# An eight-layer hybrid kernel: how one stage ends and the next begins (semaphore clears, reload of x, LayerNorm statistics)

## The chip, the cores and the metric

The kernel runs on one core of one Trainium2 chip. The metric is the device time of one execution in microseconds (us), as a median over several runs; lower is better. Five engines work side by side and meet by semaphores: PE (TensorE, the matrix unit), DVE (VectorE), ACT (ScalarE), POOL (GpSimd) and SP (SyncE, which here only issues DMAs).

## The reference

One chain of eight layers on x, 8 batches of 1024 rows with 256 elements each, all float32. Every layer adds its result to x and starts from a LayerNorm of x:

```python
x = x + _L0_attn_a_ref(_layernorm(x), ...)   # local attention
x = x + _L0_ffn_ref(_layernorm(x), ...)      # top-128 rows for each of 8 experts, two GEMMs, scatter-add
x = x + _L0_attn_b_ref(_layernorm(x), ...)   # spectral attention (DFT over 64 rows, attention, convolution)
x = x + _L0_ffn_ref(_layernorm(x), ...)      # the same experts again
x = x + _L1_attn_a_ref(_layernorm(x), ...)   # second-order linear attention
x = x + _L1_ffn_ref(_layernorm(x), ...)      # tanh(h @ W @ A1 @ A2 + bias)
x = x + _L1_attn_b_ref(_layernorm(x), ...)   # window attention
x = x + _L1_ffn_ref(_layernorm(x), ...)
```

`_layernorm` subtracts the mean of a row and divides by `sqrt(var + 1e-5)`. In the expert layer a router scores every row for 8 experts, each expert takes its best 128 rows of a batch, and `out` is added back to these rows (`.at[...].add(out)`).

## The kernel before, in words

**Stages.** The layers run one after the other, each as one stage, the two expert layers as two: `la` (local attention), `m2r` and `m2e` (router and experts), `sp` (spectral attention), `m4r` and `m4e`, `so` (second-order attention), `t6` (tanh), `wa` (window attention), `t8` (tanh, writes the output). Each is one `nc.Block()`, in which every engine has a program of its own and which ends in a barrier of all five engines. No engine enters the next stage before the last one is done.

**x and its statistics.** x stays in SBUF as `R.X`, 64 tiles (NT) of 128 rows, 8 tiles (TB) to a batch. LayerNorm is made in three steps. While a stage adds its result, DVE takes `bn_stats` of each finished tile into `R.raw` (6 numbers per row). At the start of the next stage `layernorm_scales` (L73 to L88) works on all 64 tiles at once: seven small DVE instructions, a square root on ACT (L93, behind an ACT_TABLE_LOAD), then the reciprocal and `R.shift` on DVE. Then `scaled` is counted up, and ACT or POOL normalise tile by tile.

**Experts.** The scatter-add works on a copy of x in DRAM, `sum_dram`. So `la` and `sp` store x there batch by batch (SP, counted in `x_out`), and at the end of their program SP waits until all eight stores have landed (L2424 closes the block in `la`; L909 is the store in `sp`). `m2e` runs 32 steps of pairs of batches (PAIRS = 32, 4 pairs for each of 8 experts; pair s % 4 holds batches 2s and 2s+1) in a skewed pipeline: in each step DVE first adds the second bias to item t-5 (`add_b2`, L750), weighs the same item (`weigh`, L758), and takes statistics of item t-8 (`stats`, L767). POOL scatters an item (L624) as soon as it is weighed. SP reloads `R.X` batch by batch (L593) once a batch has been scattered by all 8 experts. `stats` does something only for items 28 to 31, so all 64 `bn_stats` stand behind the last `weigh`. At the end POOL waits for all scatters.

**Semaphores.** Semaphores are scarce, so a stage hands its own back. `Stage.__exit__` (L118 to L122) does it with a second block, with its own barrier, in which POOL clears every semaphore of the stage one by one, and the other engines wait: 28 after `m2r`, 21 after `m2e` and 7 more in yet another block, 73 after `sp`, 36 after `m4r`, 21 and 7 after `m4e`, 45 after `so`, 29 after `wa`. `la`, `t6` and `t8` keep theirs and have no such block.

**What follows.** `sp` opens with twelve copies of weights, then a loop over b = -1 to 7: in step b the scores of batch b+1 are masked and reduced by DVE (L1360, L1364), exponentiated by ACT (L1184), and x of batch b+2 is normalised by ACT (L1153). `so` loops over 258 steps t; in each, DVE masks the scores (`mask_AB`, L1887) and, one item behind, `mask_P` (L1895), on which PE waits at L1677; POOL normalises two tiles ahead (L1931).

## Time and profile before

| what | us |
|---|---|
| median of 3 runs | 3836.1 (3835.32 to 3837.97) |
| the profiled execution, its own time | 3835.71 |
| its span, first to last instruction | 3833.9 |
| PE busy | 3505.2 (91%) |
| DVE busy | 2365.9 (62%) |
| ACT busy | 2113.1 (55%) |
| POOL busy | 1465.5 (38%) |
| mean granted TensorE clock | 0.962 of full speed |

The time of an execution is its span and 1.8 us around it. "Idle before, releaser" in a row is the time that the engine stood idle ahead of that instruction and what it waited for; "PEq L118" is the barrier of a clearing block (PE's queue was the last event seen), "PEq L176" and "PEq L2424" that of a block without one.

### The profile page before, as it was taken

What the parts mean: (1) busy time and instruction counts of PE and PEld (TensorE: products, weight loads), DVE (VectorE), ACT (ScalarE), POOL (GpSimd) and SP (SyncE); (2) the same over time, 40 slices, a digit from 0 to 9 for tenths busy, and PEclk for the clock granted to TensorE, in tenths of its full rate; (3) what the DMA queues carried; (4) which work ended last, traced back from release to release, by engine and by line L of the source; (5) the groups of instructions that cost most, each with busy time, mean ns of one, the idle gap of its engine ahead of it and who ended that gap; (6) DMA issues with size and microseconds to landing.
All of it is one profiled execution on the core that took longest, in us unless ns stands there. A gap on an engine that the chain in (4) does not pass through costs nothing. (4 is left out here: it accounts for less than half of the span.)

```text
span 3833.9 us, 115714 instructions
## 1 busy us (share of the span) xinstructions
PE 3505.2 (91%) x44514; PEld 3084.7 (80%) x44514; DVE 2365.9 (62%) x6483; ACT 2113.1 (55%) x6525; POOL 1465.5 (38%) x2245
## 2 busy tenths in 40 slices
PE   8948999699838999699999999999988999999998
PEld 7838999577728999699899999999976777777777
DVE  6774555588764554544444444444446888888894
ACT  3345555355445555244444444444444888888895
POOL 3444665201024665244444444444444222222215
PEclk9969999799969999899999999999999999999999
DMA  3133443411143443300000000000000000000002
GB/s 121 45 134 97 92 92 75 125 46 51 51 167 98 94 94 71 99 3 3 3 3 3 3 3 3 3 3 3 3 6 16 2 2 2 2 2 2 2 2 93
DMA packets 137901, 164.62 MB, mean 43 GB/s; under 512 B 11392, under 2 KB 127264, under 8 KB 137376
## 3 DMA queue, kind: packets, MB, share of 16 engines
q1 hardware_dynamic: 112800, 123.81, 10.0%
q0 software_dynamic: 24576, 33.57, 5.3%
q8 instruction: 359, 5.88, 0.6%
q14 instruction: 166, 1.36, 0.1%
HBM read 97.18 MB, written 60.16 MB: 41 GB/s over the span
## 5 line engine op out<-in xcount | busy, mean ns | idle before, releaser
L2249 ACT ACTIVATE wa_S<-wa_S,wa_top 128x256 f32<-128x256 f32 x1024 | 511.6, 506 | 138.9 <-DVE wa_top L2313 138.0
L1887 DVE TENSOR_TENSOR so_raw<-so_rows,so_masks 128x1024 f32<-128x1024 f32 x256 | 313.5, 1225 | 228.3 <-PE so_rows L1589 220.7
L2313 DVE CUSTOM_DVE_ANT_0 wa_S<-wa_bank,wa_band 128x256 f32<-128x256 f32 x1024 | 366.9, 420 | 8.4 <-issue 8.2
L1951 POOL TENSOR_TENSOR so_more<-so_compact,so_head 128x384 f32<-128x384 f32 x224 | 185.2, 827 | 337.2 <-PE so_bankC L1671 307.0
L2172 PE MATMUL wa_bank<-ident,wa_S 128*128 128x128 f32 x2048 | 273.9, 275 | 22.2 <-ACT wa_probT L2256 22.2
L2172 PEld LDWEIGHTS wa_bank<-ident,wa_S 128*128 128x128 f32 x2048 | 230.3, 141 | 67.1 <-ACT wa_S L2249 31.2
L1876 DVE SCALAR_TENSOR_TENSOR so_compact<-so_compact,so_bankX 128x96 f32<-128x96 f32 x192 | 48.8, 254 | 363.2 <-PE so_bankX L1707 363.2
L1805 ACT COPY so_O<-so_bankC 128x128 f32<-128x128 f32 x256 | 68.2, 266 | 307.6 <-PE so_bankC L1671 307.5
L1956 POOL TENSOR_TENSOR so_OT<-so_O,so_OT 128x128 fp32r<-128x128 f32 x256 | 117.1, 457 | 307.9 <-ACT so_OT L1811 307.9
L703 ACT ACTIVATE m4e_hT<-m_bank,m4e_bias 128x256 fp32r<-128x256 f32 x256 | 126.3, 493 | 152.2 <-PE m_bank L655 145.0
L703 ACT ACTIVATE m2e_hT<-m_bank,m2e_bias 128x256 fp32r<-128x256 f32 x256 | 126.4, 494 | 149.3 <-PE m_bank L655 142.8
L1618 PE MATMUL so_bankJ<-so_xnT,so_w 128*128 128x256 f32 x1500 | 206.6, 287 | 1.5 <-DVE so_xnT L1868 1.5
L2249 ACT ACTIVATION_READ_ACCUMULATOR wa_S<-wa_S,wa_top 128x1 f32 x1024 | 199.3, 195 | 0.0
L2321 DVE COPY wa_probT<-wa_bank 128x512 f32<-128x512 f32 x256 | 167.1, 687 | 47.8 <-PE wa_bank L2172 46.5
L655 PE MATMUL m_bank<-m4e_exT,m_w_parts 128*128 128x256 f32 x1536 | 190.5, 283 | 1.1 <-issue 1.1
L2082 POOL COPY wa_share_all<-wa_share 128x256 f32<-128x256 f32 x64 | 25.4, 396 | 434.6 <-DVE wa_share L2328 434.6
L655 PE MATMUL m_bank<-m2e_exT,m_w_parts 128*128 128x256 f32 x1536 | 189.9, 283 | 0.4 <-ACT m2e_h L703 0.4
L669 PE MATMUL m_bank<-m_w_parts,m4e_hT 128*128 128x256 f32 x1536 | 189.5, 282 | 0.6 <-DVE m4e_pre L750 0.6
L669 PE MATMUL m_bank<-m_w_parts,m2e_hT 128*128 128x256 f32 x1536 | 189.5, 282 | 0.6 <-DVE m2e_pre L750 0.6
L669 PEld LDWEIGHTS m_bank<-m_w_parts,m2e_hT 128*128 128x128 f32 x1536 | 186.3, 188 | 0.8 <-issue 0.8
L669 PEld LDWEIGHTS m_bank<-m_w_parts,m4e_hT 128*128 128x128 f32 x1536 | 186.3, 188 | 0.8 <-issue 0.8
L655 PEld LDWEIGHTS m_bank<-m4e_exT,m_w_parts 128*128 128x128 f32 x1536 | 184.7, 190 | 1.3 <-issue 1.3
(450 smaller groups left out, 10201.4 us busy)
## 6 DMA issues: line engine op xcount, KB each, us to landing
m_w_raw<-in_L_ffn_W_dram SPq DMA_DIRECT2D x64, 512.0 KB
sum_dram<-X SPq DMA_DIRECT2D x16, 1024.0 KB, 5.0
X<-sum_dram SPq DMA_DIRECT2D x16, 1024.0 KB, 6.5
X<-in_L_attn_a_x_dram SPq DMA_DIRECT2D x8, 1024.0 KB, 11.8
xn_dram<-m2r_xn SPq DMA_DIRECT2D x16, 512.0 KB, 3.7
sp_gx<-gate_dram SPq DMA_DIRECT2D x64, 128.0 KB, 2.9
xn_dram<-m4r_xn SPq DMA_DIRECT2D x16, 512.0 KB, 3.8
out_dram<-X SPq DMA_DIRECT2D x8, 1024.0 KB, 4.4
```

What stands on the lines that cost most here:

```text
L655: last = nc.tensor.matmul(bank[:, 0:2 * P], w_parts[:, par, a, c, f * P:(f + 1) * P], exT[:, s % 2, b, c], start=(n == 0), stop=(n == len( ...
L669: last = nc.tensor.matmul(by[u][:, 0:HID], hT[:, s % 2, a, f, u * P:(u + 1) * P], w_parts[:, par, b, 2 + f // QF, f % QF * HID:(f % QF + 1 ...
L703: last = nc.scalar.activation(to, bh[f % 4][:, 0:2 * P], ACT.Gelu_apprx_tanh, bias=bias[:, par, f:f + 1])
L1618: last = nc.tensor.matmul(bank[:, 2 * k * P:2 * (k + 1) * P], w[:, a, n, c, cols], xnT[:, b, c], start=(m == 0), stop=(m == 2 * len(PARTS) ...
L1805: nc.scalar.copy(O[:, t % UT], bC[:, P:2 * P]).then_inc(s_["O_copied"], 1)
L1887: nc.vector.tensor_tensor(AB[:, t % 2].rearrange("p h m t -> p h (m t)"), rows4[:, :, 0:2 * P], masks[:].rearrange("p m t -> p (m t)")[:, ...
L1951: nc.gpsimd.tensor_tensor(state[:, t % UT], compact[:, t % UT, :, None, :].broadcast_to([P, 3, HG, DK]), head[:, None, :, None].broadcast_ ...
L1956: nc.gpsimd.tensor_tensor(OT[:, 1, t % (2 * UT)], O[:, t % UT], OT[:, 0, t % (2 * UT)].bitcast(F32), ALU.subtract).then_inc(s_["O_ready"], 1)
L2172: last = nc.tensor.transpose(bT[q % 2][:, (2 * h + k) * P:(2 * h + k + 1) * P], S[:, n % 2, 2 * q + h, k * P:(k + 1) * P], R.ident[:])
L2249: nc.scalar.activation(S[:, n % 2, z], S[:, n % 2, z], ACT.Exp, bias=top[:, n % 2, z:z + 1], scale=-1.0, accum_out=sums[:, i % 2, SET * c ...
L2313: nc.vector.tensor_tensor_reduce(out=S[:, n % 2, z], in0=bS[g][:, eo * SPAN:(eo + 1) * SPAN], in1=band[:], scale=-(D ** -0.5), scalar=3e38 ...
L2321: nc.vector.tensor_copy(probT[:, n % 2, 2 * q:2 * q + 2].rearrange("p h k t -> p (h k t)"), bT[q % 2][:]).then_inc(s_["T_dve"], 1)
```

## The change

**Clears move.** `Stage.__exit__` makes no block any more. It puts the stage's semaphores on a list, and an engine of the next stage clears them in its own program by `Stage.clear_finished`: POOL in `m2r` (38, those of `la`, now a Stage too), DVE at the start of `m2e` and `m4e` (28, 36), POOL in `sp` before it zeroes `XK` (20), POOL in `m4r` (72), POOL in `so` (20; behind its waits for `loaded` and `scaled`, ahead of its first tile), POOL in `t6` (45), `wa` (12) and `t8` (29).

**The stores of x are awaited late.** `x_out` is no longer a stage's own, SP does not wait for it, and POOL waits for it at the start of `m2e` and `m4e`.

**The experts' end.** SP reloads only batches 0 to 5 in the experts' stage; 6 and 7 stand at the end of the next stage's list of loads. POOL no longer waits for all scatters. `stats` has delay 7 and acts for items 28 and 29 only, so the experts' stage takes statistics of batches 0 to 3. The rows of indices and `y`, from which the last scatters read, are no longer a stage's own.

**Late statistics.** LayerNorm is done in halves. The start of `sp` and `so` works on tiles 0 to 31 (`FIRST`). For tiles 32 to 63 (`REST`): in `sp`, DVE does 32 `bn_stats` and the seven small instructions in one piece ahead of its loop (b = -1), ACT the square root at b = 0, DVE reciprocal, shift and `R.diff` at b = 1, and ACT waits for it at b = 2. In `so`, DVE does one `bn_stats` in each of steps 16 to 47, between `mask_AB` and `mask_P`, the seven at t = 48 and the last ones at t = 50, ACT the square root at t = 49, and POOL waits for it before tile 32.

```diff
+def fetch_result(sp, R, b, before):
+    sp.wait_ge(R.scattered[b], (before + 1) * 16 * 8)
+    sp.dma_start(R.X[:, b * TB:(b + 1) * TB, :],
+                 R.sum_dram[b * SEQ:(b + 1) * SEQ, :].rearrange("(j p) d -> p j d", p=P)).then_inc(R.row_back[b], 16)
...
+    @staticmethod
+    def clear_finished(eng):
+        for sems, sem_ctx in Stage.finished:
+            for s in sems:
+                eng.sem_clear(s)
+            Stage.cleared.append(sem_ctx)
+        Stage.finished.clear()
+
     def __exit__(self, *error):
-        if not error[0] and self.sems:
-            with self.nc.Block() as block:
-                @block.gpsimd
-                def _(pool):
-                    for s in self.sems:
-                        pool.sem_clear(s)
+        for sem_ctx in Stage.cleared:
+            sem_ctx.close()
+        Stage.cleared.clear()
+        Stage.finished.append((self.sems, self.sem_ctx))
         return self.ctx.__exit__(*error)
...
-                    for b in range(BATCH):
-                        sp.wait_ge(scattered[b], 16 * E + scattered_before)
-                        sp.dma_start(R.X[:, b * TB:(b + 1) * TB, :],
-                                     summed[b * SEQ:(b + 1) * SEQ, :].rearrange("(j p) d -> p j d", p=P)).then_inc(row_back[b], 16)
+                    for b in range(BATCH - 2):
+                        fetch_result(sp, R, b, before)
...
+                    pool.wait_ge(R.x_out, 16 * BATCH * (before + 1))
                     skewed(pool, PAIRS, [(0, fetch), (3, scatter)], unroll=U)
-                    for b in range(BATCH):
-                        pool.wait_ge(scattered[b], 16 * E + scattered_before)
...
-                        if isinstance(t, int) and t >= PAIRS - PE_:
+                        if isinstance(t, int) and PAIRS - PE_ <= t < PAIRS - 2:
...
-                    skewed(dve, PAIRS, [(3, split_xT), (4, split_h), (5, add_b2), (5, weigh), (0, split_w), (8, stats)], unroll=U)
+                    Stage.clear_finished(dve)
+                    skewed(dve, PAIRS, [(3, split_xT), (4, split_h), (5, add_b2), (5, weigh), (0, split_w), (7, stats)], unroll=U)
...
+                for b in range(BATCH // 2, BATCH):
+                    dve.wait_ge(R.row_back[b], 16)
+                    for j in range(TB):
+                        ins = nc.vector.bn_stats(R.raw[:, b * TB + j, :], R.X[:, b * TB + j, :])
+                c.then(ins)
+                variances(nc, c, R, var_ready, REST)
                 for b in range(-1, BATCH):
                     u = STEPS * b
                     attend, read = b + 1 < BATCH, b + 2 < BATCH
+                    if b == 1:
+                        dve.wait_ge(std_ready, 2)
+                        scales(nc, c, R, REST)
...
+                    if STATS_AT <= t < STATS_AT + NT // 2:
+                        late = t - STATS_AT + NT // 2
+                        dve.wait_ge(R.row_back[late // TB], 32)
+                        ins = nc.vector.bn_stats(R.raw[:, late, :], R.X[:, late, :])
...
                 pool.wait_ge(s_["loaded"], 5 * 16)
                 pool.wait_ge(s_["scaled"], 1)
+                Stage.clear_finished(pool)
```

In the lists that follow, each row is an instruction (or a run of equal ones) in the order of one engine's program. A semaphore in brackets has the name of the first stage that used the same hardware semaphore, so it may read like that of another stage.

DVE at the end of `m2e`, first before, then with the change:

```order
L750 TENSOR_TENSOR m2e_pre<-m_bank,m_b 128x256 [waits m2e_y_ready,m2e_down_done]
L750 TENSOR_TENSOR m2e_pre<-m_bank,m_b 128x256 [waits m2e_y_ready]
L758 TENSOR_SCALAR m2e_y<-m2e_pre,m_gate 128x256 [waits scattered2,m2e_pre_ready]
L758 TENSOR_SCALAR m2e_y<-m2e_pre,m_gate 128x256 [waits scattered3,m2e_pre_ready]
L767 BN_STATS raw<-X 128x6 [waits m2e_row_back0]
L767 BN_STATS raw<-X 128x6 x7
L767 BN_STATS raw<-X 128x6 [waits m2e_row_back1]
```

```order
L759 TENSOR_SCALAR y<-m2e_pre,m_gate 128x256 [waits scattered1,m2e_pre_ready]
L768 BN_STATS raw<-X 128x6 [waits row_back0]
L768 BN_STATS raw<-X 128x6 x7
L768 BN_STATS raw<-X 128x6 [waits row_back1]
...
L751 TENSOR_TENSOR m2e_pre<-m_bank,m_b 128x256 [waits m2e_y_ready,m2e_down_done]
...
L759 TENSOR_SCALAR y<-m2e_pre,m_gate 128x256 [waits scattered3,m2e_pre_ready]
L768 BN_STATS raw<-X 128x6 [waits row_back2]
...
L768 BN_STATS raw<-X 128x6 [waits row_back3]
...
L587 UNCONDITIONAL_BRANCH
L1331 UNCONDITIONAL_BRANCH [waits barrier_Pool_Activation_PE_DVE_SP_release]
L76 TENSOR_TENSOR mean<-raw 128x32
```

Sixteen statistics now stand ahead of the last `add_b2`, sixteen behind it, and then DVE is in `sp`.

POOL from the end of `m4e` to its first tile of `so`, before and with the change. The second list's `m2_q_loaded2,m2_b2_ready` are `loaded` and `scaled` of `so`:

```order
L624 DMA sum_dram<-m4e_y,m4e_rows 8192x256 x2
...
L122 ISA x21
L118 UNCONDITIONAL_BRANCH
L119 UNCONDITIONAL_BRANCH [waits barrier_Pool_Activation_PE_DVE_SP_gather]
L122 ISA x7
L118 UNCONDITIONAL_BRANCH
L1923 UNCONDITIONAL_BRANCH [waits barrier_Pool_Activation_PE_DVE_SP_gather]
L1931 TENSOR_SCALAR so_xn<-X,rstd,shift 128x256 [waits sp_g_stored,sp_q_done]
```

```order
L626 DMA sum_dram<-y,rows 8192x256 x2
L587 UNCONDITIONAL_BRANCH
L1960 UNCONDITIONAL_BRANCH [waits barrier_Pool_Activation_PE_DVE_SP_gather]
L137 ISA [waits m2_q_loaded2,m2_b2_ready]
L137 ISA x19
L1971 TENSOR_SCALAR so_xn<-X,rstd,shift 128x256 x2
```

The 28 clears between barriers are gone; 20 stand between the wait for `loaded` and the first tile.

ACT in `sp`, from the end of step b = -1 to the exponential of step b = 0, with the change:

```order
L1213 ACTIVATE sp_gel<-sp_acc 128x8x28 [waits la_pT_ready]
L103 ACT_TABLE_LOAD
L103 ACTIVATE var<-var 128x32 [waits sp_var_ready]
L1157 ACTIVATE sp_xn<-X,shift,rstd 128x256 [waits sp_f_done] x8
L1188 ACT_TABLE_LOAD
L1188 ACTIVATE sp_late<-sp_late 128x1024 [waits sp_shifted]
```

The two rows at L103 are new; the rest stood there before (as L1209, L1153 and L1184).

## Rows read from the trace of the kernel before

**Rows 1.** Timeline, DVE: a block that ends in its barrier alone (t6 to wa).
```profile
2922.55 0.27 DVE L77 TENSOR_TENSOR mean<-raw 128x64 f32<-128x64 f32 x1 [0.30 <-PEq L176]
```
**Rows 2.** Timeline, end of m2e, start of sp; then PE at the start of so.
```profile
686.14 0.76 DVE L750 TENSOR_TENSOR m2e_pre<-m_bank,m_b 128x256 f32<-128x256 f32 x2 [5.32 <-PE m_bank L669]
687.34 21.00 DVE L767 BATCH_NORM_STATS2 raw<-X 128x6 f32<-128x256 f32 x64
710.93 0.27 DVE L77 TENSOR_TENSOR mean<-raw 128x64 f32<-128x64 f32 x1 [2.60 <-PEq L118]
...
1572.60 8.75 PE L1712 MATMUL so_bankC<-ident 128*128 128x128 f32 x60 [24.83 <-PEq L118]
```
**Rows 3.** Timeline, first instructions of m2e, m4e, t6 and t8 behind clears.
```profile
291.21 0.21 DVE L726 TENSOR_SCALAR m2e_bias<-m_b 128x8 f32<-128x8 f32 x1 [2.36 <-PEq L118]
...
1149.54 0.21 DVE L726 TENSOR_SCALAR m4e_bias<-m_b 128x8 f32<-128x8 f32 x1 [3.16 <-PEq L118]
...
2846.80 0.27 DVE L77 TENSOR_TENSOR mean<-raw 128x64 f32<-128x64 f32 x1 [3.75 <-PEq L118]
...
3753.42 0.27 DVE L77 TENSOR_TENSOR mean<-raw 128x64 f32<-128x64 f32 x1 [2.71 <-PEq L118]
```
**Rows 4.** Timeline, start of m2r, behind la's last store of x.
```profile
235.90 0.17 DVE L484 MEMSET m2r_ones<- 128x128 f32 x1 [3.38 <-PEq L2424]
...
238.99 0.29 PEld L373 LDWEIGHTS m_bank<-ident,m2r_wg_rows 8*128 8x128 f32 x2 [9.46 <-DMA m2r_rowbase<-in_row_base_dram]
```
**Rows 5.** Timeline, end of sp and start of m4r.
```profile
1083.76 0.38 SPq L909 DMA_DIRECT2D sum_dram<-X  x1
...
1086.09 0.18 ACT L1238 COPY L<-sp_bank 128x32 f32<-128x32 f32 x1 [0.42 <-PE sp_bank L1082]
...
1093.58 1.28 ACT L93 ACT_TABLE_LOAD   x1 [7.31 <-PEq L118]
```
**Rows 6.** Timeline, what stands idle where clears go: DVE in m2e, POOL before m4e.
```profile
301.74 0.69 DVE L732 CAST m2e_exT<-m_bank 128x512 fp32r<-128x512 f32 x1 [10.33 <-PE m_bank L640]
...
1149.53 0.20 POOL L606 TENSOR_TENSOR m4e_rows<-m_index,m_zero 128x2 uint32<-128x2 uint32 x1 [7.86 <-POOLq L118]
```
**Rows 7.** Reload of x in m2e: two issues in the timeline, and landing times.
```profile
685.11 2.22 SPq L593 DMA_DIRECT2D X<-sum_dram  x2
...
DMA to landing us min/median/max: 5.6/7.0/7.9
```
**Rows 8.** Timeline, sp: the first ACT instruction and step b = -1.
```profile
715.80 0.20 ACT L1242 ACTIVATE sp_alpha<-sp_alpha 128x1 f32<-128x1 f32 x1 [0.85 <-DMA sp_alpha<-_L_attn_b_alpha_raw_dram]
...
744.33 0.69 DVE L1360 SCALAR_TENSOR_TENSOR sp_late<-sp_bank,sp_mask 128x512 f32<-128x512 f32 x1 [9.90 <-PE sp_bank L988]
...
747.21 1.23 DVE L1364 TENSOR_TENSOR sp_late<-sp_late,sp_tops 128x1024 f32<-128x1024 f32 x1
...
750.75 1.04 ACT L1184 ACTIVATE sp_late<-sp_late 128x1024 f32<-128x1024 f32 x1
```
**Rows 9.** Timeline, sp, step b = 0: PE behind the normalise, and a table load.
```profile
770.90 2.14 PE L927 MATMUL sp_bank<-sp_dft,sp_xn 128*128 128x128 f32 x16 [1.36 <-ACT sp_xn L1153]
...
774.19 1.28 ACT L1184 ACT_TABLE_LOAD   x1
```
**Rows 10.** Timeline, so: POOL's first tile, then one step of the loop.
```profile
1582.15 1.09 POOL L1931 TENSOR_SCALAR so_xn<-X,rstd,shift 128x256 f32<-128x256 f32 x2 [29.23 <-DMA so_head<-in_head_dram]
...
1659.72 0.68 DVE L1895 TENSOR_TENSOR so_raw<-so_rows,so_masks 128x512 f32<-128x512 f32 x1
...
1661.30 0.43 PE L1677 MATMUL so_bankU<-so_raw,so_KW 128*32 128x128 f32 x8
```
**Rows 11.** Windows: us, then busy of PE, PEld, DVE, ACT, POOL; PEclk, DMA share, GB/s.
```profile
717.00:723.00 6.00, 5.87 (x27) 5.90 (x28) 1.76 (x3) 3.53 (x7) 1.59 (x3) 0.50 1.08 367
...
1613.00:1670.00 57.00, 57.00 (x1092) 52.73 (x1085) 27.20 (x42) 26.05 (x91) 28.55 (x45) 1.00 0.01 3
```
**Rows 12.** The page's row of the granted TensorE clock, in 40 slices.
```profile
PEclk9969999799969999899999999999999999999999
```

More of the change, by code:

```diff
@@ new lines, in scales, with layernorm_scales, std_of_var @@
+def scales(nc, c, R, tiles=slice(0, NT)):
+    c.then(nc.vector.reciprocal(R.rstd[:, tiles], R.var[:, tiles]))
+    c.then(nc.vector.tensor_tensor(R.shift[:, tiles], R.mean[:, tiles], R.rstd[:, tiles], ALU.mult))
+def layernorm_scales(nc, dve, R, step, var_ready, std_ready, tiles=slice(0, NT)):
+    c = Chain(dve, step)
+    variances(nc, c, R, var_ready, tiles)
+    dve.wait_ge(std_ready, 1)
+    scales(nc, c, R, tiles)
+    return c
+def std_of_var(nc, act, R, var_ready, std_ready, tiles=slice(0, NT), count=1):
+    act.wait_ge(var_ready, count)
+    nc.scalar.activation(R.var[:, tiles], R.var[:, tiles], ACT.Sqrt).then_inc(std_ready, 1)
@@ L570, in top_k_experts @@
             bias_ready = ex.sem("bias_ready")
-            row_back = [ex.sem(f"row_back{b}") for b in range(BATCH)]
             bx, bh, by = ban[0], ban[1:5], ban[6:8]
@@ L891, in _ @@
                 sp.dma_start(wg_rows[:], A["L0_ffn_Wg"]).then_inc(wg_loaded, 16)
+                for b in range(BATCH - 2, BATCH):
+                    fetch_result(sp, R, b, 0)
                 for b in range(BATCH + 1):
@@ L1522, in second_order_attention @@
         s_ = {n: sem(n) for n in names}
+        FIRST, REST = slice(0, NT // 2), slice(NT // 2, NT)
+        STATS_AT = 4 * UT
         def tile(t):
@@ L1564, in _ @@
                     sp.dma_start(to, C[name]).then_inc(s_["loaded"], 16)
+                for b in range(BATCH - 2, BATCH):
+                    fetch_result(sp, R, b, 1)
             @block.tensor
@@ L2736, in hybrid_kernel @@
 def hybrid_kernel(nc, A, C, out):
+    Stage.finished.clear()
+    Stage.cleared.clear()
     with ExitStack() as ctx:
@@ L2745, in hybrid_kernel @@
         R.fetched = [sem(f"fetched{n}") for n in range(4)]
+        R.row_back = [sem(f"row_back{b}") for b in range(BATCH)]
+        R.x_out = sem("x_out")
+        R.rows, R.y = sb("rows", [P, BATCH, 2], U32), sb("y", [P, 2, 2, HID])
         R.scattered = [sem(f"scattered{b}") for b in range(BATCH)]
```

111 lines of the change are left out of this document (56 added, 55 removed).

## The prediction, made before the change was run

> **What bounds the kernel now.** I read the windows first. In the loop of `so`, PE is busy for 57.00 of 57.00 us while DVE works for 27.20 and the DMA engines for 1% [rows 11]; over the whole span PE is at 91% (the table of times). Inside the stages PE is the bound and nothing in the change makes its work shorter. So I went to the places where PE stands still, and read the timeline around each change of stage: the reader is to look at the time in brackets, idle time ahead of the first instruction. At the start of `so` PE had been idle for 24.83 us, and its releaser is a barrier [rows 2]. These seams are what the change can win.
>
> **The price of a bare barrier and of a clear.** t6 to wa has no clearing block, and DVE starts 0.30 us after its last instruction [rows 1]. Where 28, 36 and 45 semaphores are cleared in between, the idle time is 2.36, 3.16 and 3.75 us [rows 3]. With two barriers (0.6) taken off that is 1.76/28 = 0.063, 2.56/36 = 0.071 and 3.15/45 = 0.070 us for a clear; I take 0.067.
>
> **Savings at the plain seams.** Each falls to a bare 0.30: m2r to m2e 2.36 - 0.30 = 2.1; m4r to m4e 3.16 - 0.30 = 2.9; so to t6 3.75 - 0.30 = 3.45; wa to t8 2.71 - 0.30 = 2.4 [rows 3]. Together 10.85.
>
> **la to m2r.** DVE idles 3.38 us behind its last instruction, since SP holds the barrier until the last store of x has landed [rows 4]. Without that wait 3.38 - 0.30 = 3.1. But PE in `m2r` first waits for a load, `m2r_rowbase` [rows 4], and the loads are now issued while 1 MB is still being stored. I take 2.7 (1.8 to 3.1).
>
> **sp to m4r.** The last store is issued at 1083.76, the last work on ACT ends at 1086.27, and ACT goes on at 1093.58, after 7.31 us: the landing of the store, then 73 clears at 0.067 = 4.9 [rows 5]. All goes but 0.3: 7.0.
>
> **End of the experts, twice.** DVE ends its statistics at 687.34 + 21.00 = 708.34 and begins `sp` at 710.93 [rows 2]; one of them costs 21.00/64 = 0.328. Sixteen now stand ahead of the last `add_b2`, where DVE was idle for 5.32 us: 16 x 0.328 = 5.25, hidden. Their reloads are long there, since item 29 was scattered 11 us earlier. Sixteen follow the last `weigh`: 687.34 + 5.25 = 692.6. POOL issues its last scatter until 691.3 and no longer waits. So `sp` begins at 692.6 + 0.3 = 692.9 instead of 710.93, and nearly the same rows stand at the end of m4e: about 17.9 each, 35.8 for both.
>
> Sum of savings: 10.85 + 2.7 + 7.0 + 35.8 = 56.35 us.
>
> **Where clears are put.** In `m2e` and `m4e` DVE does 28 and 36 at the start (1.9 and 2.4 us), ahead of an idle time of 10.33 us [rows 6]. In `m2r` 38 on POOL take 2.5 us while the scales are being made, some 3.2 us. In `m4r` 72 take 4.8, about 1.4 later than `scaled`, but POOL had been idle for 7.86 us at that stage's end [rows 6] and only writes `xn`: 0 (up to 1.4 if the last store of `xn` then lands after DVE's index work). In `sp`, `t6`, `wa` and `t8` POOL has nothing due in that time. In `so` there is no cover: the 20 clears stand between `loaded` and POOL's first tile, which now starts the moment that `so_head` has landed [rows 10], with PE waiting on it: 20 x 0.067 = 1.3.
>
> **Costs at the start of sp.** SP queues its loads while the reload of batches 4 and 5 (issued at 685.11 and after, 7 us to landing [rows 7]), the scatters of 6 and 7, and then their reload are under way. ACT's first instruction waits on a load [rows 8]. I add 0.5 (0 to 2). In step b = -1, DVE must put 32 x 0.328 = 10.5 and seven small instructions (at some 0.23 each, less than the 0.27 of [rows 2], 1.6) into the 9.90 us in which it waits for the first scores [rows 8]: 2.2 too long. But DVE's last step there ends at 748.44 and ACT, which takes it, is busy until 750.75 [rows 8], so 2.3 of delay fit: 0.2 (0 to 2.3). In step b = 0 ACT gets the square root and a table load (1.28 as in [rows 9], and 0.26) ahead of its normalise, on which PE already waits for 1.36 [rows 9]: 1.55. DVE's three instructions at b = 1: 0.5 (0 to 1). Sum 2.75.
>
> The row of the table load shows 1.28 us at 774.19, and the exponential that needs it starts at 775.49, right behind it [rows 9]. The Trainium skill, "ScalarE: Activation LUTs", section "What ACT_TABLE_LOAD costs", gives about 1283 ns and a drain of about 1380 ns, 2.66 us for a switch. By that page the sum would be 1.4 us higher, and the time 3786; the trace shows no drain behind this one.
>
> **Costs in so.** Its loads meet the same reloads: 1.0 (0 to 2). The clears: 1.3. The late statistics: one `bn_stats` before `mask_P` in 32 of 258 steps. `mask_P` (L1895) ends at 1660.40 and PE takes it at 1661.30, with no idle time of its own [rows 10], so 0.9 us of slack stand against 0.33. The bound from above is that PE was ready for it: 32 x 0.33 and the 2.7 of the small instructions = 13. The chain of seven at t = 48 and three at t = 50, 1.6 and 1.1 us at once, is over the slack: 0.5. Sum 2.8.
>
> **Net.** 56.35 - 2.75 - 2.8 = 50.8. The profiled execution took 3835.7, so 3784.9; the median lies 0.4 above it: **3785 us**.
>
> **Rivals.**
> (A) As above, 3785, its own range 3783 to 3792. For it: every saving is read from a barrier's own idle time, and PE is the engine that waits there.
> (B) All costs hidden: the loads land in time and the slack in `sp` and `so` holds. Only the 20 clears and the table load remain, 2.9 us: 3836.1 - 56.35 + 2.9 = 3782.7, and with 3.1 for la, 3782. With nothing exposed at all it is 3779.8.
> (C) The change doesn't do what it says: a block still ends only when the DMAs that its engines issued are done. Then la loses its 2.7, sp to m4r the landing (2.0), and each end of the experts runs on to the landing of the last scatters, some 2.5 later: about 10 us, 3795. Against it: the instruction lists show nothing but the barrier there. For it: no row of before shows a barrier with a DMA under way, since t6 has none [rows 1].
> (D) The late statistics are not hidden but only moved. In `sp` the reload of batch 7 comes late and the whole block of 12 us lies on the path; in `so` the 32 cost their 13. That is 24 us: 3809. Against it: the slack in [rows 8] and [rows 10], and DVE at 27.20 of 57 [rows 11].
> (E) Slower than before: PE's clock. At the start of `so` PE does a burst of 60 transposes of the identity, 8.75 us at 1572.60 [rows 2], and then idles until POOL's first tile at 1582.15 [rows 10], 2 us. The clears and the crowded loads lengthen this to some 4.3 us. PE is busy without a pause in the loop behind it [rows 11], so if the granted clock fell from 2.4 to the 1.2 GHz level there and stayed, each us of PE's work would take two: the gain is gone once that lasts for over 51 us of its work, and 80 us would give 3785 + 80 = 3865. Against it: at the start of `sp`, after a pause far longer, the clock stood at 0.50 for 6 us (717 to 723) and the loop of `so` ran at 1.00 [rows 11]; in the page's row no slice of 96 us lies below 0.6 and each one that does lie at 0.6 is followed by 0.9 [rows 12].
>
> The same with rows alone: if the pause of 4.3 us does lower the clock and it comes back as in `sp`, 6 us at 0.50 cost 3 us, and the time is 3788, inside A. The Trainium skill, "TensorE: Matmul & The Clock Gate", section "HAM oscillation — how this bites in real kernels", speaks against this part of the change: a wait for a DMA between two bursts lets the array fall back to half its clock, and the next burst starts cold. The short pause of before did not do that lastingly, for the loop runs at 1.00 [rows 11]; no run here shows the longer one.
>
> **Chances.** A 0.73, B 0.10, C 0.07, D 0.06, E 0.04. The likeliest is A, 3785. The range takes in the bounds: all costs at their lower end give 3779.8; the small ones at their upper end (2 + 2.3 + 1.55 + 1 in `sp`, 2 + 1.3 + 1 in `so`, 1.4 in `m4r`, 0.9 for la) are 13.5 in place of 5.6 and give 3793, and C gives 3795. With a us or two for the price of a clear: 3778 to 3797. A measurement of this kernel can tell about 0.2% (8 us) from no change. Faster by more than that: A, B, C and nearly all of D (at 3809 it is still 27 us faster), 0.94. Within: 0.03, the clock low for some 50 us, or D with losses of its kind in other stages. Slower: 0.03, the rest of E.
>
> **What the profile after would show.** Right: DVE's idle time before its first LayerNorm instruction (the L77 of before) near 0.3 at every change of stage; 16 `bn_stats` in the gap before the last `add_b2`; `sp` beginning some 7 us after that `add_b2`, not 25; PE still at 57 of 57 in the loop of `so`. C is seen in a barrier wait of 2 us and more where x was stored. D is seen in DVE waiting for `row_back` in `sp`, and in PE waiting for `so_raw` at L1677 in steps 16 to 47. E is seen in a granted clock near 0.5 behind the burst and into the loop. The forecast falls with whichever of them is the larger: 24.83 us of PE's idle time before `so` that shrink by less than 17, or a loss of over 8 us inside `sp` or `so`.

## The result, and the profile after

The changed kernel takes 3797.5 us (median of 4 runs, 3795.73 to 3799.22) beside 3836.6 us (4 runs, 3835.32 to 3837.97): a ratio of 0.990, 95% interval 0.9888 to 0.9913. It is 39.1 us faster. The prediction said 3785, and its range, 3778 to 3797, ended half a microsecond below the measured time. The direction was right, the size was 12 us too large.

The profiled execution has a span of 3793.8 us, 40.1 below the 3833.9 of before. The start of each stage is the first LayerNorm instruction on DVE (for `m2r` and `m4r` the memset ahead of it, for `m2e` and `m4e` POOL's first instruction). From start to start, in us, with the change that the prediction's terms add up to:

| stage | before | changed | measured | forecast |
|---|---|---|---|---|
| up to m2r (la) | 235.9 | 233.1 | -2.8 | -2.7 |
| m2r | 55.3 | 53.3 | -2.0 | -2.1 |
| m2e | 419.7 | 407.0 | -12.8 | -17.9 |
| sp | 382.8 | 377.5 | -5.3 | -4.3 |
| m4r | 55.9 | 54.4 | -1.4 | -2.9 |
| m4e | 423.1 | 411.3 | -11.8 | -17.9 |
| so | 1274.2 | 1275.2 | +1.0 | -0.7 |
| t6 | 75.8 | 74.0 | -1.7 | 0 |
| wa | 830.9 | 827.3 | -3.6 | -2.4 |
| t8 | 80.5 | 80.7 | +0.2 | 0 |
| sum | | | -40.1 | -50.8 |

So the gap is at the two ends of the experts' stages (11.2 of it), in `m4r` (1.5) and in `so` (1.7); elsewhere 3.7 came on top.

The seams that carry nothing but a barrier now do what was forecast. Timeline of the changed kernel, first instructions of `m2r`, `m4r`, `t6` and `t8` (start, us, instruction, idle time before it and what ended it; they answer to [rows 3 to 5]):

```profile
233.14 0.17 DVE L488 MEMSET m2r_ones<- 128x128 f32 x1 [0.36 <-PEq L2464]
...
1070.76 1.28 ACT L103 ACT_TABLE_LOAD   x1 [0.27 <-PEq L883]
...
2811.77 0.28 DVE L76 TENSOR_TENSOR mean<-raw 128x64 f32<-128x64 f32 x1 [0.32 <-PEq L1578]
...
3713.11 0.28 DVE L76 TENSOR_TENSOR mean<-raw 128x64 f32<-128x64 f32 x1 [0.30 <-PEq L2077]
```

The 3.38, 7.31, 3.75 and 2.71 us of before are 0.36, 0.27, 0.32 and 0.30.

The end of `m2e` does not. Timeline of the changed kernel, DVE, then SP, then POOL, answering to [rows 2]:

```profile
676.32 5.32 DVE L768 BATCH_NORM_STATS2 raw<-X 128x6 f32<-128x256 f32 x16
681.66 0.76 DVE L751 TENSOR_TENSOR m2e_pre<-m_bank,m_b 128x256 f32<-128x256 f32 x2
...
682.86 5.32 DVE L768 BATCH_NORM_STATS2 raw<-X 128x6 f32<-128x256 f32 x16
693.41 0.22 DVE L76 TENSOR_TENSOR mean<-raw 128x32 f32<-128x32 f32 x1 [5.24 <-PEq L587]
...
680.62 2.28 SPq L109 DMA_DIRECT2D X<-sum_dram  x2
...
685.24 1.55 POOL L626 DMA_INDIRECT sum_dram<-y,rows  x1 [0.30 <-issue]
693.38 0.15 POOL L1479 MEMSET sp_wgT<- 128x64 f32 x1 [6.60 <-POOLq L587]
```

The sixteen statistics fit into the gap ahead of the last `add_b2`, as forecast, and DVE is done at 688.18. Then everybody waits: SP has issued its last reload at 682.9, POOL its last scatter at 686.79, and the barrier opens at 693.4. DVE idles for 5.24 us where 0.3 was forecast, and the end of `m4e` shows 5.38. In windows of 1 us the traffic stops before the barrier opens (us, then busy time of PE, PEld, DVE, ACT, POOL, granted clock, DMA share, GB/s):

```profile
689.00:690.00 1.00, 0.00 (x0) 0.00 (x0) 0.00 (x0) 0.00 (x0) 0.00 (x0) 0.50 1.19 250
690.00:691.00 1.00, 0.00 (x0) 0.00 (x0) 0.00 (x0) 0.00 (x0) 0.00 (x0) 0.50 0.74 131
691.00:692.00 1.00, 0.00 (x0) 0.00 (x0) 0.00 (x0) 0.00 (x0) 0.00 (x0) 0.50 0.08 12
692.00:693.00 1.00, 0.00 (x0) 0.00 (x0) 0.00 (x0) 0.00 (x0) 0.00 (x0) 0.50 0.00 0
```

The trace also names who is late. At a block's end it has an instruction named `DRAIN` for an engine, and the barrier opens when the last of these has ended. Neither a timeline nor the lists of instructions above show it, but the view of one line does (L587 here is the barrier of the experts' block; the numbers are the duration in ns, three times the same, then the start in us). The changed kernel:

```profile
L587 SPq DRAIN  x1: 123/123/123, 683.0 to 683.0; - x1
L587 POOLq DRAIN  x1: 10145/10145/10145, 683.0 to 683.0; - x1
L587 DVEq DRAIN  x1: 3922/3922/3922, 684.3 to 684.3; - x1
```

SP's takes 0.12 us, although two of its reloads have not landed. DVE's ends at 688.2, with its statistics. POOL's ends at 693.1, 6.3 us after its last instruction, and the barrier opens behind it. At the end of `m4e` it ends 6.5 us after.

At the start of `so`, PE after its burst, and POOL ahead of it (answering to [rows 2, 10]):

```profile
1536.56 8.56 PE L1735 MATMUL so_bankC<-ident 128*128 128x128 f32 x60 [11.94 <-PEq L587]
...
1548.54 1.10 POOL L1971 TENSOR_SCALAR so_xn<-X,rstd,shift 128x256 f32<-128x256 f32 x2 [18.76 <-issue]
...
1549.79 0.71 PE L1634 MATMUL so_bankJ<-ident,so_xn 128*128 128x128 f32 x4 [4.67 <-POOL so_xn L1971]
...
1552.02 2.93 PE L1641 MATMUL so_bankJ<-so_xnT,so_w 128*128 128x256 f32 x12 [1.53 <-DVE so_xnT L1893]
```

POOL's first tile comes 11.98 us after the stage's start instead of 9.55, PE's pause is 4.67 us instead of 2.04, and the twelve matmuls at 1552.02 take 2.93 us.

### The profile page after: what moved, and what is told of

Its sections match the earlier page's. It is cut to its first block and busy times, and to the rows that moved or that the text cites. A ratio compares the mean times of both kernels' runs of the same rounds, so it can differ in the third digit from the quotient of the medians.

```text
span 3793.8 us, 115662 instructions
## 1 busy us (share of the span) xinstructions
PE 3506.4 (92%) x44514; PEld 3086.2 (81%) x44514; DVE 2371.0 (62%) x6503; ACT 2117.6 (56%) x6528; POOL 1471.5 (39%) x2245
## 5 line engine op out<-in xcount | busy, mean ns | idle before, releaser
L626 POOL DMA_INDIRECT sum_dram<-y,rows x128 | 223.5, 1746 | 29.4 <-issue 27.2
L656 PEld LDWEIGHTS m_bank<-m2e_exT,m_w_parts 128*128 128x128 f32 x1536 | 188.5, 191 | 0.0
L1641 PEld LDWEIGHTS so_bankJ<-so_xnT,so_w 128*128 128x128 f32 x1500 | 185.3, 190 | 1.8 <-DVE so_xnT L1893 1.8
```

Of the source, the lines that this page charges most:

```text
L626: nc.gpsimd.indirect_dma_start(out=summed, out_offset=bass.IndirectOffsetOnAxis(ap=rows[:, s, u:u + 1], axis=0), in_=y[:, s % 2, u, :], in ...
L656: last = nc.tensor.matmul(bank[:, 0:2 * P], w_parts[:, par, a, c, f * P:(f + 1) * P], exT[:, s % 2, b, c], start=(n == 0), stop=(n == len( ...
L1641: last = nc.tensor.matmul(bank[:, 2 * k * P:2 * (k + 1) * P], w[:, a, n, c, cols], xnT[:, b, c], start=(m == 0), stop=(m == 2 * len(PARTS) ...
```

## The experiments

All are compared with the kernel before on the same chip; the medians are of 4 runs or more where an interval is given, else one execution is told. The stage times come from one profiled execution each.

### The last scatter in the next stage

POOL issues the scatter of item 31 as its first work of `sp` and `so`:

```diff
+def scatter_last(nc, R):
+    for u in range(2):
+        nc.gpsimd.indirect_dma_start(out=R.sum_dram[:, :], out_offset=bass.IndirectOffsetOnAxis(ap=R.rows[:, BATCH - 1, u:u + 1], axis=0),
+                                     in_=R.y[:, 1, u, :], in_offset=None, compute_op=ALU.add
+                                     ).then_inc(R.scattered[BATCH - 2 + u], 16)
...
                     def scatter(t, s):
+                        if isinstance(t, int) and t == PAIRS - 1:
+                            return
```

> The changed kernel, but POOL issues the scatter of the last item (batches 6 and 7) as its first work in the next stage (sp, so), not as its last in the experts' stage. In the changed kernel DVE ended its statistics at 688.18 and sp began at 693.41, 5.24 us later (5.38 at the start of so), though PE, ACT and SP had nothing left to issue. Theory 1: a block's end waits until POOL's scatters under way are done. Then both seams fall to 0.3 to 1 us, and the time from 3797.5 by some 10 to about 3788 (up to 1 more for the later reload of batches 6 and 7). Theory 2: what holds the barrier is SP's reload of batch 5, which is still landing at about 691. Then nothing changes: 3797.5. Theory 3: POOL pays a fixed time at a block's end after any scatter, counted from its last instruction; then the seams fall too, since its last one is now 6.5 us earlier.

Measured: 3787.9 us, ratio 0.987 (0.9853 to 0.9886); before ran at 3838.1 there. The profile is of the slowest of the four executions, 3794.1 us. Timeline, DVE at the end of `m2e`, then POOL:

```profile
685.82 5.32 DVE L777 BATCH_NORM_STATS2 raw<-X 128x6 f32<-128x256 f32 x16
691.44 0.21 DVE L76 TENSOR_TENSOR mean<-raw 128x32 f32<-128x32 f32 x1 [0.30 <-PEq L594]
...
692.03 1.55 POOL L108 DMA_INDIRECT sum_dram<-y,rows  x1 [8.84 <-POOLq L594]
```

Both seams are 0.30 us, `m2e` falls from 407.0 to 401.2 and `m4e` from 411.3 to 405.3. SP's reload of batches 4 and 5 was under way as before and holds nothing: theory 2 is out. It is POOL's scatter. POOL's `DRAIN` in this kernel:

```profile
L594 POOLq DRAIN  x1: 7491/7491/7491, 679.4 to 679.4; - x1
```

It ends at 686.9, 3.7 us after the scatters of item 30, and so 4.2 us before DVE is done. The wait is still there; it is only no longer the last.

### The reload of batches 4 and 5 in the next stage

```diff
-                    for b in range(BATCH - 2):
+                    for b in range(BATCH - 4):
                         fetch_result(sp, R, b, before)
...
-                for b in range(BATCH - 2, BATCH):
+                for b in range(BATCH - 4, BATCH):
                     fetch_result(sp, R, b, 0)
```

> The changed kernel, but SP reloads only batches 0 to 3 in the experts' stage; 4 to 7 follow the next stage's loads. POOL's last scatter stays where it is. Theory 2 (SP's reload holds the barrier): the seams fall from 5.24 and 5.38 us to 0.3, and the time to about 3788. Theory 1 (POOL's scatter holds it): a wait remains; if it ends with the landing, it is 1 to 3 us shorter, since the scatter no longer shares the DMA engines with 2 MB of reload, and the time is 3792 to 3796; if it is a fixed time it stays at 5.2 and 5.4: 3797.5.

Measured: 3792.2 us, ratio 0.9881 (0.9865 to 0.9898). Both seams are 2.75 us. POOL's timeline:

```profile
683.37 1.55 POOL L626 DMA_INDIRECT sum_dram<-y,rows  x1 [0.30 <-issue]
689.03 0.15 POOL L1479 MEMSET sp_wgT<- 128x64 f32 x1 [4.11 <-POOLq L587]
```

A wait remains although no reload is under way, but it is 2.5 us shorter: the traffic is over at 687.0, not at 691.1. POOL's own idle time is 4.11 us. The time alone would not show the gain, since its interval overlaps the changed kernel's; the seams do.

### Work on POOL behind the scatter

```diff
                     skewed(pool, PAIRS, [(0, fetch), (3, scatter)], unroll=U)
+                    nc.gpsimd.memset(hT[:, 0].rearrange("p a f t -> p (a f t)").bitcast(F32), 0.0)
```

> The changed kernel with one memset of 128x4096 on POOL (some 3.5 us) behind the last scatter of each experts' stage. Theory 1 (the block's end waits for the scatter): the memset runs while the scatter is under way, the seams stay near 5.2 and 5.4 us and the time near 3797. Theory 3 (a fixed time of 6.5 us after POOL's last instruction): both seams grow by some 3.5, to 8.7 and 8.9, and the time to about 3804.

Measured: 3796.7 us in one execution, with a seam of 6.28 us at `sp` and the same at `so`. POOL's timeline:

```profile
685.83 4.09 POOL L632 MEMSET m2e_hT<- 128x4096 f32 x1
694.03 0.15 POOL L1480 MEMSET sp_wgT<- 128x64 f32 x1 [4.11 <-POOLq L587]
```

Neither theory 1 (no change) nor theory 3 (3.5 us more) holds as written: the memset ends 3.5 us after the scatter's issue did, and the seams grow by 1.0 and 0.9. Together with the run above a simple form fits: POOL at the end of an experts' block takes 4.11 us from its last instruction to its next one if its scatters are down or nearly so, to the hundredth in both kernels, and longer if they are still landing among 2 MB of reloads: 6.60 us in the changed kernel, 6.1 to 7.3 in five other kernels with the same end of `m2e`.

The trace of the kernel before bears this out. There POOL's program waits until all its scatters have landed (696.0), and only then comes its `DRAIN`; beside it, that of POOL at the end of `t6` in the changed kernel, where it has issued no DMA:

```profile
L583 POOLq DRAIN  x1: 3859/3859/3859, 696.2 to 696.2; - x1
```
```profile
L179 POOLq DRAIN  x1: 831/831/831, 2884.3 to 2884.3; - x1
```

The first takes 3.86 us with nothing in flight. It was hidden, since DVE worked until 708.3. The second ends 0.07 us after POOL's last instruction. So the 3.9 us do not wait for a landing; they come with the indirect DMAs issued just before, and with reloads under way they are more.

### Without the late statistics

```diff
-                        ins = nc.vector.bn_stats(R.raw[:, late, :], R.X[:, late, :])
                         if late == NT - 1:
+                            ins = nc.vector.bn_stats(R.raw[:, late, :], R.X[:, late, :])
                             c.then(ins)
```

and the same for the block of 32 in `sp`, of which one is left.

> The changed kernel without 31 of the 32 late statistics in sp and without 31 of the 32 in so (the LayerNorm of batches 4 to 7 there is then computed from old statistics; all else is the same). The prediction's theory: they are almost all hidden, sp gains 0 to 2 us and so 0 to 1.5, so 3794 to 3797.5. Rival D: they displace work one for one, so sp gains 10 and so 10: about 3777.

Measured: 3797.0 us, ratio 0.989 (0.9874 to 0.9907), against 3797.5 and 0.990 with them. They cost nothing that can be seen: the one profile has 378.5 us for `sp` and 1277.5 for `so`, no less than with them. Rival D is out.

### Clears moved away from POOL's first tile

In `so` behind the first two tiles, in `m2r` and `m4r` from POOL to PE:

```diff
                 pool.wait_ge(s_["loaded"], 5 * 16)
                 pool.wait_ge(s_["scaled"], 1)
-                Stage.clear_finished(pool)
...
                 normalize(0)
                 normalize(1)
+                Stage.clear_finished(pool)
...
+                    Stage.clear_finished(pe)
                     pe.wait_ge(r_["valued"], 2)
```

> The changed kernel with nothing moved but the clears: in so behind the first two tiles (still behind the wait for the constants), in m2r and m4r from POOL to PE. The prediction put 1.3 us on the clears in so and 0 (up to 1.4) on those in m4r. If that is their price, POOL's first tile in so comes 10.7 us after the stage's start instead of 11.98, and m4r is 1.5 us shorter (52.9 instead of 54.43): 3794.7 in all. If the last store of xn holds m4r for another reason, m4r stays at 54.4.

Measured: 3787.0 us in one execution, 7.7 below what was expected. 5.3 us of the gain stand in `m4e` (406.0), in whose program nothing was moved; that part is not explained by the clears. In `so`, PE:

```profile
1541.12 0.63 PE L1634 MATMUL so_bankJ<-ident,so_xn 128*128 128x128 f32 x4 [1.88 <-POOL so_xn L1970]
1543.27 1.67 PE L1641 MATMUL so_bankJ<-so_xnT,so_w 128*128 128x256 f32 x12 [1.53 <-DVE so_xnT L1893]
```

The stage began at 1530.09, so POOL's first tile (1539.88) came after 9.79 us, 2.2 earlier than in the changed kernel, and `so` fell by 4.0 us, to 1271.2. DVE's first mask of the loop came 20.6 us after the stage's start instead of 25.1, so 2.3 us more were won between the tile and the loop. They go with the clock. Windows of the stretch behind the burst, the kernel before, the changed kernel, then this one:

```profile
1583.30:1590.60 7.30, 5.67 (x33) 5.46 (x34) 1.92 (x2) 2.49 (x4) 1.09 (x2) 0.77 0.00 0
```
```profile
1549.70:1557.00 7.30, 5.69 (x27) 5.40 (x28) 1.92 (x2) 2.12 (x3) 1.10 (x2) 0.53 0.21 67
```
```profile
1541.00:1548.40 7.40, 5.76 (x48) 5.55 (x49) 1.92 (x2) 3.29 (x5) 1.09 (x2) 1.00 0.49 157
```

After a pause of 4.67 us the granted clock stands at 0.53 of full speed (near the 1.2 GHz level) and PE does 27 matmuls in 7.3 us; after one of 1.88 us it stands at 1.00 (2.4 GHz) and PE does 48 in 7.4. The kernel before, with a pause of 2.04 us, lies between: 0.77 and 33. The twelve matmuls take 1.67 us instead of 2.93 (2.06 before).

`m4r` did not get shorter (55.1 us, 54.4 in the changed kernel): the 72 clears on POOL were not what held it.

### Clears and stores alone

All reloads and all 64 statistics at the experts' end, as before; the rest of the change stays:

```diff
-                    for b in range(BATCH - 2):
+                    for b in range(BATCH):
                         fetch_result(sp, R, b, before)
...
-                        if isinstance(t, int) and PAIRS - PE_ <= t < PAIRS - 2:
+                        if isinstance(t, int) and PAIRS - PE_ <= t:
...
-        FIRST, REST = slice(0, NT // 2), slice(NT // 2, NT)
+        FIRST = slice(0, NT)
```

> The other half of the change alone: clears in the next stage, x_out awaited late, but all eight reloads and all 64 statistics at the experts' end as before, LayerNorm in one piece, no late statistics. By the seams of the profile: la 2.8, m2r 2.0, m4r 1.4, sp 7.0, wa 2.4, so 3.4 less 1.3 for the clears, and 2.3 at each experts' end, where POOL's scatter has long landed behind 21 us of statistics: 22.3, so about 3814 beside 3836.6 of before. If POOL's scatter held the barrier by a fixed time or SP's reload did, the experts' ends would keep their wait: the seam there would be over 2 us, not 0.3.

Measured: 3813.7 us, ratio 0.9941 (0.9924 to 0.9957). Forecast for it was 3814. Timeline, DVE:

```profile
681.32 21.00 DVE L768 BATCH_NORM_STATS2 raw<-X 128x6 f32<-128x256 f32 x64
702.62 0.27 DVE L76 TENSOR_TENSOR mean<-raw 128x64 f32<-128x64 f32 x1 [0.30 <-PEq L587]
```

With 17 us between POOL's last scatter and its next work, the seam is 0.30. So this half of the change is worth some 23 us, and the moved reloads and statistics the other 16. It also gives the price of the late part inside `sp`: 374.0 us here, 377.5 in the changed kernel, 3.4 more. And it answers for the loads at the start of `so`: no reload is under way there, and still the constants land 10.0 us after the stage's start and POOL's first tile comes after 11.73 (10.2 and 11.98 in the changed kernel, 9.5 and 9.55 before).

### The stores awaited again

```diff
                                      R.X[:, (b - 1) * TB:b * TB, :]).then_inc(R.x_out, 16)
+                sp.wait_ge(R.x_out, 32 * BATCH)
```

and the same with 16 in `la`.

> The changed kernel with SP waiting again for the stores of x at the end of la and of sp. The prediction gave la's wait 2.7 us and sp's 2.1 (7.31 of idle time less 73 clears): the seam at m2r goes from 0.36 back to about 3.4 us and m2r loses its shorter start, the seam at m4r from 1.60 to about 3.6; the time is 4.8 us longer. If a hardware store under way did hold the barrier by itself, as POOL's scatter does, nothing would change.

Measured: 3805.8 us in one execution; the seams are 3.38 us at `m2r` and 3.67 at `m4r`, as against 0.36 and 1.60: 3.0 and 2.1 us. The stores of SP do not hold a barrier unless SP waits for them. The other 3.2 us of the total are not explained; `t6`, which this edit does not touch, is alone 2.9 longer.

### The kernel before, 64 bytes higher

```diff
+        R.pad = sb("pad", [P, 16])
         R.X = sb("X", [P, NT, HID])
```

> The kernel before with nothing but 64 unused bytes per partition ahead of x in SBUF, so that x and every later tile stand 64 bytes higher. In every run of the changed kernel's family the router's stores of xn (512 KB each) landed after a median of 4.3 to 4.8 us, before after 3.8, and the reload of x after 7.2 to 7.8, before after 6.5; the change had put 64 bytes of indices ahead of x. If the place in SBUF is the reason, the stores of xn go from 3.8 to some 4.6 us here too, the reload from 6.5 to 7.3, the end of m4r comes up to 1.5 us later, and the time is 0 to 3 us above before (some 3838). If contention with other transfers is the reason, nothing moves: 3.8, 6.5 and 3836.5.

Measured: 3837.0 us (10 runs) beside 3835.8 (13 runs), ratio 1.0007 (0.9997 to 1.0017). The page's rows of the router's stores (KB each, median us to landing), before, then shifted:

```profile
xn_dram<-m2r_xn SPq DMA_DIRECT2D x16, 512.0 KB, 3.7
xn_dram<-m4r_xn SPq DMA_DIRECT2D x16, 512.0 KB, 3.8
```
```profile
xn_dram<-m2r_xn SPq DMA_DIRECT2D x16, 512.0 KB, 4.5
xn_dram<-m4r_xn SPq DMA_DIRECT2D x16, 512.0 KB, 4.7
```

A shift of 64 bytes in SBUF alone makes these stores 0.8 us slower, and `m4r` grows from 55.85 to 57.42 us, all of it in the wait behind DVE's last instruction. That is the size of the 1.5 us missing in the changed kernel, but each is one profile, and in profiles of kernels whose program for `m4r` is the same it takes 54.2 to 56.8 us. `m2r`, with the same slower stores, does not grow (55.0 us, 55.3 before). The reload of x stays at a median of 6.5 over both stages (from 6.2 to 6.4 in `m2e`, from 6.5 to 7.4 in `m4e`). In the changed kernel it is 7.8; contention with the late reloads is not shown as the reason, since the kernel with clears alone has 7.5.

### The changed kernel, aligned as before

```diff
-        R.rows, R.y = sb("rows", [P, BATCH, 2], U32), sb("y", [P, 2, 2, HID])
...
         R.L = sb("L", [P, NT, 8])
+        R.y, R.rows = sb("y", [P, 2, 2, HID]), sb("rows", [P, BATCH, 2], U32)
...
+            pad = rt.sb("pad", [P, 112])
             xn = rt.sb("xn", [P, RING, HID])
```

> The changed kernel with the indices and y behind x in SBUF (x stands where it did before) and 448 unused bytes ahead of the router's xn, so that both have their old place within 512 bytes. If the place is the reason: stores of xn 3.8 us, m4r 53.0 instead of 54.43 us, the reload of x near 6.6, so that POOL's scatter also lands earlier and the seams at sp and so fall from 5.24 and 5.38 to some 4.5: about 3795. If contention is the reason: no row moves, 3797.5.

Measured: 3793.4 us, ratio 0.9893 (0.9876 to 0.9909), on a chip where before took 3835.8. The stores of xn land after 3.7 and 4.1 us, `m4r` takes 53.6 us (0.8 of the 1.5 is back), the seams are 5.04 and 5.20. The ratio cannot be told from the changed kernel's own; the rows of the stores moved as expected, `m4r` by half of it, and the seams by less than they differ between kernels with the same end of `m2e` (4.7 to 5.9).

### No table load in sp

```diff
-                        std_of_var(nc, act, R, var_ready, std_ready, REST, 2)
+                        act.wait_ge(var_ready, 2)
+                        nc.scalar.copy(R.var[:, REST], R.var[:, REST]).then_inc(std_ready, 1)
```

> The changed kernel with the square root of tiles 32 to 63 in sp replaced by a copy on ACT, which needs no table (the LayerNorm of batches 4 to 7 in sp is then computed from the variance in place of its root). The prediction charged 1.28 us for the table load; the trace shows nothing between its end and the next instruction. If that is its price, sp falls by 1.3 us, from 377.45 to about 376.1; if a drain of 1.38 us belongs to it, to 374.8; if it is hidden, it stays.

Measured: 3797.4 us in one execution, `sp` 377.3. By the total it is hidden, but the total misleads. The exponential of step b = 0 starts 63.0 us after the stage's start, in the changed kernel 64.4, in the kernel with clears alone 62.9. So the load costs 1.4 us (the other nine profiles that have it lie at 64.3 to 65.7, so 1.3 at least). Here it is given back by b = 2, where the granted clock is lower than in the changed kernel (0.91 against 0.96 from 80 to 120 us after the start). The changed kernel's rows, ACT:

```profile
750.63 1.28 ACT L103 ACT_TABLE_LOAD   x1
751.93 0.23 ACT L103 ACTIVATE var<-var 128x32 f32<-128x32 f32 x1
752.07 1.08 ACT L1157 ACTIVATE sp_xn<-X,shift,rstd 128x256 f32<-128x256 f32 x2
```

Here too nothing stands between the load and the next instruction. The drain of 1.38 us that the Trainium skill, "ScalarE: Activation LUTs", section "What ACT_TABLE_LOAD costs", adds to each switch is not seen, neither in these rows nor in the 1.4 us.

### Two combined kernels

The first takes the scatter of the first experiment, the clears on PE, and in `so` the first two tiles ahead of the clears and of the wait for the constants.

> The last scatter of each experts' stage is issued in the next stage (as in e1), the 72 clears of m4r and the 38 of m2r go from POOL to PE, which idles for 12 us while DVE searches, and in so POOL normalises its first two tiles as soon as the scales are there, ahead of the 20 clears and of the wait for the constants. If the clears cost what stands in the changed kernel's trace (POOL's first tile 1.3 us late in so, m4r's end 1.57 us late), m4r falls from 54.4 to 52.9, and in so the first tile goes to about 4 us after the start and PE takes it right behind its burst, some 9 us after the start instead of 13.2: 3 to 4 us if the weights are there by then, 1.5 if not. With e1 (3788): 3782 to 3786. Against it: if PE's own clears delay the search's transposes, m2r and m4r grow; if the clock at the start of so falls anyway, so gains under 1.

Measured: 3787.7 us, ratio 0.987 (0.9849 to 0.9891), a miss. The seams are 0.30, but `so` takes 1274.5 us. PE in `so` waits for the constants itself, and these land later (11.5 us after the stage's start, 10.2 in the changed kernel). POOL's scatters now run among the loads, as in the first experiment, where it was 11.8:

```profile
1537.35 1.11 PE L1644 MATMUL so_bankJ<-ident,so_xn 128*128 128x128 f32 x4 [2.42 <-DMA so_head<-in_head_dram]
```

The second puts the scatters behind the first loads, lets PE, ACT and DVE wait for the constants only ahead of their loops, and is aligned:

```diff
                 ins.then_inc(diag_ready, 1)
 
+                scatter_last(nc, R)
                 Stage.clear_finished(pool)
...
                 normalize(0)
                 normalize(1)
+                pool.wait_ge(s_["loaded"], 5 * 16)
+                scatter_last(nc, R)
+                Stage.clear_finished(pool)
...
-                pe.wait_ge(s_["loaded"], 5 * 16)
                 turn_x(0)
```

> The changed kernel, aligned as in e10, with the last scatter of each experts' stage issued in the next stage, but there only after the first loads have landed (behind the taps in sp, behind the first two tiles and the constants in so); in so POOL's first tiles, PE's first transposes, ACT and DVE no longer wait for the constants, only the loop does, and the clears stand behind the first tiles. Seams 0.3 (10 us), m4r 1.5, and at the start of so no pause of PE behind its burst and so no drop of the granted clock: 4 to 5 us. From 3797.5 that gives 3779 to 3783. If later scatters and reloads delay the statistics of batches 6 and 7 in sp, DVE waits for row_back there and it is 3785 or more.

Measured: 3779.0 us (3776.33 to 3779.96) beside 3835.8, ratio 0.9853 (0.9837 to 0.987). Its interval lies wholly below the changed kernel's: it beats both. Both seams are 0.30, `so` takes 1269.2 us, and PE goes from its burst into the first tile with no pause:

```profile
1525.52 9.44 PE L1746 MATMUL so_bankC<-ident 128*128 128x128 f32 x60 [6.85 <-PEq L595]
1534.80 0.60 PE L1645 MATMUL so_bankJ<-ident,so_xn 128*128 128x128 f32 x4
1536.80 1.67 PE L1652 MATMUL so_bankJ<-so_xnT,so_w 128*128 128x256 f32 x12 [1.40 <-DVE so_xnT L1902]
```

## Why the prediction was wrong in size

**End of the experts, twice (35.8 forecast, 24.6 measured).** This is the step that failed. The prediction wrote "POOL issues its last scatter until 691.3 and no longer waits", and gave the block's end to DVE. POOL does wait: its program has no wait left, but its `DRAIN` ends 6.3 and 6.5 us after its last instruction, the issue of a scatter, 4.9 and 5.1 after DVE was done. Rival C named the place, with 0.07 and "some 2.5 later". It was right that POOL's scatters lengthen the block, but its 2.5 us were half of what came (4.94 and 5.08), and it was wrong for SP's stores, whose seams fell as in A. Its reason was only in part right: of the 6.3 us, 3.9 are there with nothing in flight.

The arguments against C were weak ones. The list of instructions shows no such wait because it leaves out the `DRAIN`. And "no row of before shows a barrier with a DMA under way" did not need such a row: POOL's `DRAIN` of 3.86 us stood in the trace of before, under DVE's 21 us of statistics. Against a DVE that ends at 688.2, POOL's last scatter at 686.8 and those 3.9 us already give some 2.5 of the 4.9.

The other 1.1 us are in `m4e`. The granted clock was 0.98 in 100 us of it (1.00 before), but the first experiment has the same 0.98 and 405.3 us, and `m4e` also differed by 5 us where nothing in it had been moved; what made the 1.1 is open.

**m4r (2.9 forecast, 1.4 measured).** The clears were hidden, as forecast; the bound "up to 1.4 if the last store of `xn` lands after DVE's index work" came true in size. The likely reason is one that the prediction had not: `R.rows`, 64 bytes, was put ahead of x, and everything behind it moved. That this makes the stores slower is shown. That it makes the stage longer is seen in one profile of the kernel before (1.57 us); in the changed kernel the old alignment gave 0.8 back, and in the combined one `m4r` took 54.6 although its stores landed after 3.7 us, so the cause of the 1.5 stays open.

**Inside so (2.8 of costs forecast, 4.4 measured).** 3.2 of it stand ahead of the loop (first mask 25.1 us after the stage's start, 21.9 before). The clears were forecast at 1.3 and cost 1.6: POOL's first tile comes 1.75 us behind the landing of the constants, 0.10 before. The landing itself is 0.8 later, forecast at 1.0 for the crowded loads; but with no reload in the way it was 0.6 later too, so the crowd is not shown to be the reason. The rest, 0.8, goes with the clock: PE's pause of 4.67 us (forecast 4.3) was followed by 0.53 of full speed, that of 2.04 us before by 0.77. The prediction had this as the small form of rival E, at 3 us and with a time of 3788, and left it out of the sum; it took the short pause of before as harmless, and it was not wholly so. The large form, a clock that stays low in the loop, did not come: the loop stands at 1.00. The other 1.2 us are lost in the loop, by the late part of LayerNorm (below).

**sp (2.75 of costs forecast; measured 1.7 at first sight, 3.4 beside the kernel with clears alone).** Step by step: the block of 32 in b = -1 was forecast at 0.2 and costs 0 (the exponential starts 38.9 us after the stage's start with it and without); the table load and square root were forecast at 1.55 and cost 1.4 to 1.5; the three instructions at b = 1, 0.5, cost 0 (39.6 us from b = 0 to b = 1 in both kernels). Another 2 us come at b = 2 and 3, with a dip of the clock. Against before, 1 us is won at the start.

**Late statistics in so.** The 32 `bn_stats` were forecast as hidden, and are. The small instructions at t = 48 and 50, forecast at 0.5, cost more. From the first mask of the loop to the 131st, at about step 65, the kernel before takes 315.1 us and the one with clears alone 315.3; the changed kernel takes 316.5, and so does the one without the statistics.

**The plain seams (10.85), la (2.7), sp to m4r (7.0).** Except for `m4r`'s end, told above, the barriers fell as forecast, to 0.4 us each, by a bare barrier's 0.30 and 0.067 for a clear. On top came 1.7 us in `t6` and 1.2 in `wa`. Those in `t6` are luck: PE started it at full clock after a pause of 1.23 us (4.67 before, at the lower clock), but ten of the eleven other kernels with such a pause took 75.6 to 76.9 us, about as before's 75.8 or more. The 1.2 in `wa` are no more than kernels with the same seam differ in it (827.2 to 829.7). Without these 2.9 us the forecast would have missed by more.

## What to carry to other kernels

A barrier opens when the last engine's `DRAIN` has ended, which can be microseconds behind that engine's last instruction. Before work is taken off the end of a block, look at each engine's `DRAIN` there, also at those now hidden behind a slower engine. Here it was POOL's, behind indirect DMAs in the block's last microseconds, and it was cured by issuing the last of them in the next block, best behind that block's first loads. And where a small buffer is added to the resident ones, put it last: what stands behind it moves, and here its stores became 0.8 us slower.
